# Eight of 26 embedding fields picked on chip in a four-tile interaction network, with a new tile schedule

## What is computed

```
e  = stack([tbl_f[ids[:, f]] for f in range(26)], axis=1)          # 512 x 26 x 32
x1 = einsum('bik,bjk,hij->bhk', e,  e, W1) + b1[None, :, None]     # 128 maps
x2 = einsum('bik,bjk,hij->bhk', x1, e, W2) + b2[None, :, None]     # 128 maps
z  = sum(concatenate([x1, x2], axis=1), axis=-1)                   # 512 x 256
h  = relu(concatenate([z, dense_ctx], axis=1) @ W_top1 + b_top1)   # 512 wide
h  = relu(h @ W_top2 + b_top2)                                     # 256 wide
y  = h @ W_top3                                                    # 512 x 1
```

## Time and profile before

| | |
|---|---|
| timed, median of 3 | 188.49 us |
| the profiled execution, span of the core | 269.0 us |
| PE busy, 1239 matmul records | 171.1 us |
| ACT / DVE / POOL busy | 103.7 / 94.1 / 109.4 us |
| mean granted TensorE clock | 0.797 |

### The profile page before, as it was taken

How to read it: one execution, slowest core, us unless ns; L and a number is a source line. 1 busy time by engine, 2 the same in 40 slices (tenths; PEclk the granted TensorE clock), 3 DMA queues, 4 the chain that set the end, 5 groups by cost and what they waited for, 6 DMA issues and landing times.

```text
span 269.0 us, 3544 instructions
## 1 busy us (share of the span) xinstructions
PE 171.1 (64%) x1239; PEld 158.7 (59%) x1239; DVE 94.1 (35%) x370; ACT 103.7 (39%) x267; POOL 109.4 (41%) x110
## 2 busy tenths in 40 slices
PE   7900594209929388986300799954001999899997
PEld 7800583209729287976300789954002999888985
DVE  0576003210943086920000568500003569047200
ACT  1020330019595165494000462951003463966313
POOL 3778777720077400577774003877770000000000
PEclk9975598556997869996555599995555799999999
DMA  6700011000001000011000000001000000000000
GB/s 240 250 12 13 12 14 14 13 7 0 0 10 17 11 1 4 2 12 15 14 12 10 0 0 2 11 12 15 12 12 2 0 0 0 0 0 0 0 0 3
DMA packets 5729, 5.08 MB, mean 19 GB/s; under 512 B 2875, under 2 KB 5061, under 8 KB 5718
## 3 DMA queue, kind: packets, MB, share of 16 engines
q0 software_dynamic: 3328, 1.71, 4.7%
q1 hardware_dynamic: 1698, 2.34, 2.6%
q10 hardware_dynamic: 692, 0.89, 1.0%
HBM read 4.93 MB, written 0.00 MB: 18 GB/s over the span
## 4 chain that ended last, share of the span: by engine, by line
PE 35%; another core or an unknown queue 30%; ACT 15%; DVE 9%; issue 9%; POOL 0%; DVEq 0%; ACTq 0%; POOLq 0%
PE bank L321 9%; ACT diag L467 8%; PE bank L287 4%; DVE t L650 4%; PE bank L322 4%; PE bank L281 4%; PE bank L256 3%; PE bank L332 2%; DVE prod L771 2%; PE bank L372 1%; ACT w2t L432 1%; ACT t L486 1%; DVE prod L616 1%; PE bank L275 1%
## 5 line engine op out<-in xcount | busy, mean ns | idle before, releaser
L242 POOL DMA_INDIRECT rows<-in_tbl_dram,idx x104 | 108.7, 1045 | 91.1 <-DVE prod L616 57.4
L321 PE MATMUL bank<-diag,prod 128*128 128x108 f32 x256 | 60.7, 336 | 56.0 <-DVE t L650 44.3
L321 PEld LDWEIGHTS bank<-diag,prod 128*128 128x128 f32 x256 | 46.6, 227 | 59.5 <-issue 59.5
L650 DVE COPY t<-bank 13x64 f32<-13x64 f32 (+2 forms) x128 | 26.7, 209 | 108.6 <-ACT t L487 66.7
L322 PE MATMUL bank<-diag,prod 128*77 128x64 f32 x256 | 41.7, 249 | 0.3 <-issue 0.3
L322 PEld LDWEIGHTS bank<-diag,prod 128*77 128x77 f32 x256 | 36.8, 173 | 0.5 <-issue 0.5
L485 ACT COPY t<-bank 55x128 f32<-55x128 f32 x32 | 8.3, 259 | 71.9 <-remote 47.8
L467 ACT COPY diag<-prod 32x416 f32<-32x416 f32 (+2 forms) x48 | 33.4, 696 | 1.0
L287 PE MATMUL bank<-w1ab,w2t 128*128 128x169 f32 x52 | 16.0, 489 | 14.6 <-ACT folded L434 9.7
L287 PEld LDWEIGHTS bank<-w1ab,w2t 128*128 128x128 f32 x52 | 12.8, 278 | 17.5 <-ACT folded L434 10.4
L281 PE MATMUL bank<-w1s,w2t 128*128 128x183 f32 x52 | 10.8, 377 | 16.4 <-ACT w2t L432 15.6
(11 more groups left out here) (79 smaller groups left out, 186.3 us busy)
## 6 DMA issues: line engine op xcount, KB each, us to landing
rows<-in_tbl_dram,idx POOLq DMA_INDIRECT x104
wt<-in_W_top_dram SPq DMA_DIRECT2D x2, 512.0 KB
w<-in_L_rec_W_dram ACTq DMA_DIRECT2D x1, 832.0 KB
w<-in_L_rec_W_dram SPq DMA_DIRECT2D x1, 832.0 KB
w<-in_L_rec_W_dram SPq DMA_DIRECT2D x1, 338.0 KB
idx<-in_ids_dram SPq DMA_DIRECT2D x4, 13.0 KB
vec<-in_L_rec_b_dram ACTq DMA_DIRECT2D x2, 0.5 KB
dctx<-in_dense_ctx_dram ACTq DMA_DIRECT2D x1, 32.0 KB
```

The source lines that it names most:

```text
L242: pool.indirect_dma_start(rows[:, f, :], None, tables[f], bass.IndirectOffsetOnAxis(ap=idx[i][:, f:f + 1], axis=0)).then_inc(s_got[part], 16)
L321: nc.tensor.matmul(m0[:, g * P:g * P + JW * QUADS], prod[:, G, 0:P], mov, start=True, stop=True)
L650: ins = nc.vector.tensor_copy(t1[p0:p0 + HALF, GRAM + slot:GRAM + slot + nb, n].rearrange("p j (g r) -> p j g r", r=QUADS), m1[64:64 + HAL ...
```

## The change

What it does:

- Fields are reordered (ORDER) so that eight fields with 1000 or 1250 rows stand at positions 0 to 3 and 13 to 16 (SMALL). They are no longer gathered. Their tables are loaded whole (`small`, 128 x 2240 floats, row number modulo 128 on the partitions). PE spreads the low seven bits of the ids over the partitions (`broadcast`, eight matmuls of 512 columns), DVE compares them with the partition number (`onehot`), and for each tile `look_up` multiplies one-hot by table, six banks a tile (widths 512, 512, 256, 320, 320, 320). DVE's `pick` multiplies each bank by a mask (`chosen`) and reduces over the 8 or 10 chunks into `rows[t]`.
- POOL gathers 18 fields a tile, 72 in all, into four separate buffers. It waits for nothing of DVE, but after every third gather (BURST), and at the end of a part, until they have landed.
- The weights come from memory in the layout that is needed (`w1p`, `w1t`, `w2t`, `vec`, `dctx` are permuted copies), so PE's transposes of `w2`, of `w1ab`, `w1s`, `vec` and `dctx` and DVE's strided sums go; one add gives `w1s` and one `z1w`.
- `diag` is laid out (group, quadrant, field) instead of (group, field, quadrant). For the first two parts ACT fills it over all 128 partitions with a per-partition scale of 0 or 1 (`spread`, four instructions a part); the third part is filled by DVE with four small copies.
- `factor`, a copy of the fields, lies in PSUM (bank 6), and the products read one factor from there.
- Moments go in four steps of eight groups over two sets of three banks, and are read out of PSUM with a stride of 32 or 16 floats (`evict`, `bands`).
- The loops are written out. The dense layers of tile t stand ahead of the moments of tile t + 1, which wait for `s_y`. Ahead of the last tile PE runs 12 matmuls that nobody reads (`keep_clock`).

The diff, cut to its core:

```diff
-GSTEP = 4
+GSTEP = 8
 STEPS = GROUPS // GSTEP
+GBANK = 4
+NBANK = GBANK * QUADS
 NSTEP = GSTEP * QUADS
+GPROD = 4
+PRODS = GROUPS // GPROD
 COL_A = P + 64
 COL_B = COL_A + HALF
 PCOLS = COL_B + HALF + WRAP
...
+SMALL = [0, 1, 2, 3, 13, 14, 15, 16]
+CHUNKS = [8, 8, 8, 8, 8, 10, 10, 10]
+MAXC = max(CHUNKS)
+SPLACE = [EMB * sum(CHUNKS[:e]) for e in range(len(SMALL) + 1)]
+PICKS = [(0, 2), (2, 4), (4, 5), (5, 6), (6, 7), (7, 8)]
+CROWS = P
+CBITS = 7
+NEEDS = [2, 6, 6]
+WARM = 6
+FILL = 12
 D_CTX = 16
...
-        MOM = [(bank[0], bank[1]), (bank[2], bank[3])]
-        Z1, Z2 = bank[4], bank[5]
-        L1 = [bank[6], bank[7], bank[2], bank[3]]
-        L2, L2_LAST = bank[6:8], bank[4:6]
-        L3 = bank[6]
-        s_w1, s_w2, s_vec, s_ctx, s_wt = (sem(n) for n in ("s_w1", "s_w2", "s_vec", "s_ctx", "s_wt"))
+        Z1, Z2 = bank[0], bank[7]
+        L1 = [bank[3], bank[4], bank[5], bank[7]]
+        L2, L3 = bank[0:2], bank[2]
+        ARRIVE = [[6, 7, 6, 7, 6, 7], [1, 2, 3, 4, 5, 1]]
+        LATE = [bank[3], bank[4], bank[5], bank[7]]
...
+            for t in range(TILES):
+                if t < 2:
+                    pool.wait_ge(s_idx[t], 16)
+                for part, (_, f1, _, g0) in enumerate(PARTS):
+                    for f in range(g0, f1):
+                        if f > g0 and (f - g0) % BURST == 0:
+                            pool.wait_ge(s_got[t][part], 16 * (f - g0))
+                        pool.indirect_dma_start(
+                            rows[t][:, f, :], None, tables[f],
+                            bass.IndirectOffsetOnAxis(ap=idx[:, t, f:f + 1], axis=0)).then_inc(s_got[t][part], 16)
+                    pool.wait_ge(s_got[t][part], 16 * (f1 - g0))
...
+            def broadcast():
+                pe.wait_ge(s_place, 1)
+                for e in range(len(SMALL)):
+                    nc.tensor.matmul(bank[e][:], with_dims(ident[0:len(SMALL), e:e + 1], (0, P)), placef[:],
+                                     start=True, stop=True).then_inc(s_bc, 1)
+            def look_up(t, picks):
+                for pick in picks:
+                    e0, e1 = PICKS[pick]
+                    ps = bank[ARRIVE[t > 0][pick]]
+                    if t == 0 and pick >= 2:
+                        pe.wait_ge(s_pick, pick - 1)
+                    elif t and pick == 5:
+                        pe.wait_ge(s_pick, t * len(PICKS) + 1)
+                    for e in range(e0, e1):
+                        c = slice(SPLACE[e] - SPLACE[e0], SPLACE[e + 1] - SPLACE[e0])
+                        mm = nc.tensor.matmul(ps[:, c], onehot[:, e, t * P:(t + 1) * P],
+                                              small[:, SPLACE[e]:SPLACE[e + 1]], start=True, stop=True)
+                    mm.then_inc(s_em, 1)
...
+                    b0 = 3 * (s % 2)
+                    if s == 1 and t:
+                        pe.wait_ge(s_h1, t * MT1)
                     if s >= 2:
                         pe.wait_ge(s_e0, t * STEPS + s - 1)
                         pe.wait_ge(s_eg, t * STEPS + s - 1)
                     for g in range(GSTEP):
                         G = s * GSTEP + g
-                        mov = diag[:, G, :, :].rearrange("p j r -> p (j r)")
-                        nc.tensor.matmul(m0[:, g * P:g * P + JW * QUADS], prod[:, G, 0:P], mov, start=True, stop=True)
-                        mm = nc.tensor.matmul(m1[0:M1, g * J1 * QUADS:(g + 1) * J1 * QUADS], prod[:, G, P:P + M1],
-                                              mov[:, JLOW * QUADS:], start=True, stop=True)
+                        if G % GPROD == 0:
+                            pe.wait_ge(s_pb, t * PRODS + G // GPROD + 1)
+                        m0 = bank[b0 + g // GBANK][:].rearrange("p (g r j) -> p g r j", g=GBANK, r=QUADS)
+                        m1 = bank[b0 + 2][0:M1, :].rearrange("p (g r j) -> p g r j", g=GSTEP, r=QUADS)
+                        nc.tensor.matmul(m0[:, g % GBANK, :, 0:JW], prod[:, G, 0:P], diag[:, G, :, :], start=True, stop=True)
...
+            broadcast()
+            for q in range(DONE["ctB"]):
+                make(q)
+            pe.wait_ge(s_oh, len(SMALL))
+            pe.wait_ge(s_small, 16)
+            look_up(0, (0, 1))
+            for q in range(DONE["ctB"], DONE["v1"]):
+                make(q)
+            look_up(0, (2, 3, 4, 5))
+            pe.wait_ge(s_sf, DONE["v1"])
+            for t in range(TILES):
+                if t:
+                    pe.wait_ge(s_y, t)
+                if t == TILES - 1:
+                    keep_clock(t)
                 moments(t)
+                if t < TILES - 1:
+                    pe.wait_ge(s_e0, t * STEPS + 3)
+                    pe.wait_ge(s_eg, t * STEPS + 3)
+                    look_up(t + 1, (0, 1))
+                pe.wait_ge(s_e0, t * STEPS + STEPS)
+                pe.wait_ge(s_eg, t * STEPS + STEPS)
+                if t == 0:
+                    for q in range(DONE["v1"], len(SETUP)):
+                        make(q)
+                    pe.wait_ge(s_sf, len(SETUP))
+                    pe.wait_ge(s_vec, 32)
+                    pe.wait_ge(s_wt, 48)
+                if t < TILES - 1:
+                    look_up(t + 1, (2, 3, 4))
+                z2_low()
+                if t < TILES - 1:
+                    look_up(t + 1, (5,))
+                z2_high()
+                if t == 0:
+                    pe.wait_ge(s_z1w, 1)
+                z1()
+                if t < TILES - 1:
+                    pe.wait_ge(s_pick, (t + 2) * len(PICKS))
+                layer1(t)
+                layer2(t)
+                layer3(t)
...
+            def evict(t):
                 for s in range(STEPS):
+                    b0 = 3 * (s % 2)
+                    act.wait_ge(s_mom, t * STEPS + s + 1)
+                    if s == 0 and t:
+                        act.wait_ge(s_z1, t)
+                    n0 = s * NSTEP
+                    def low(p0, p, slots, js):
+                        src = bank[b0 + 2][0:p, :].rearrange("p (n j) -> p j n", n=NSTEP)[:, js]
+                        dst = t1[p0:p0 + p, slots, n0:n0 + NSTEP]
+                        return nc.scalar.copy(dst, src)
+                    low(0, C1, slice(0, GRAM), slice(0, J1, 2))
+                    low(64, C1, slice(0, GRAM - 1), slice(1, J1 - 1, 2))
+                    low(0, C1, slice(GRAM, GRAM + 1), slice(J1 - 1, J1))
+                    for b in range(GSTEP // GBANK):
+                        src = bank[b0 + b][:].rearrange("p (n j) -> p j n", n=NBANK)[:, 0:JW]
+                        n = n0 + b * NBANK
+                        ins = nc.scalar.copy(t0[:, :, n:n + NBANK], src)
+                    ins.then_inc(s_e0, 1)
+            def spread(t, part):
+                f0, f1, col, _ = PARTS[part]
+                act.wait_ge(s_turn[part], t + 1)
+                for r in range(QUADS):
+                    ins = nc.scalar.activation(diag[:, :, r, f0:f1], prod[:, :, col:col + f1 - f0], ACT.Identity,
+                                               scale=quad[:, r:r + 1])
+                ins.then_inc(s_diag, 1)
...
+            for part in range(LATE_PART):
+                spread(0, part)
+            for t in range(TILES):
+                evict(t)
+                if t == 0:
+                    for q in range(DONE["v1"], len(SETUP)):
+                        take(q)
+                    act.wait_ge(s_vec, 32)
+                if t < TILES - 1:
+                    spread(t + 1, 0)
+                act.wait_ge(s_z2, t + 1)
+                nc.scalar.activation(z[1][:], Z2[:, 0:P], ACT.Identity, bias=b2x32[:, 0:1]).then_inc(s_z2s, 1)
+                act.wait_ge(s_z1, t + 1)
+                nc.scalar.copy(z[0][:], Z1[:, 0:P]).then_inc(s_z1s, 1)
                 relu1(t)
+                relu2(t)
+                copy_y(t)
+                if t < TILES - 1:
+                    spread(t + 1, 1)
...
+            def pick(t):
+                if t == 0:
+                    dve.wait_ge(s_ch, 1)
+                for i, (e0, e1) in enumerate(PICKS):
+                    n, cs = e1 - e0, CHUNKS[e0]
+                    width = n * EMB * cs
+                    dve.wait_ge(s_em, t * len(PICKS) + i + 1)
+                    if t or i:
+                        dve.wait_ge(s_sum, t * len(PICKS) + i)
+                    nc.vector.tensor_tensor(
+                        picked[:, 0:width].rearrange("p (f k c) -> p f k c", f=n, c=cs),
+                        bank[ARRIVE[t > 0][i]][:, 0:width].rearrange("p (f k c) -> p f k c", f=n, c=cs),
+                        with_dims(chosen[:, t, e0, 0:1], (MAXC, n), (0, EMB), (1, cs)), ALU.mult).then_inc(s_pick, 1)
+                    dve.wait_ge(s_pick, t * len(PICKS) + i + 1)
+                    nc.vector.tensor_reduce(rows[t][:, SMALL[e0]:SMALL[e0] + n, :],
+                                            picked[:, 0:width].rearrange("p (f k c) -> p f k c", f=n, c=cs),
+                                            mybir.AxisListType.X, ALU.add).then_inc(s_sum, 1)
...
```

(26 more changed lines are left out.)

635 lines of the change are left out of this document (280 added, 355 removed).

## The result

The changed kernel takes 201.57 us (median of 4 runs, 200.36 to 202.46), the kernel before 188.15 (187.78 to 188.94): a ratio of 1.070, 95% interval 1.064 to 1.076. The forecast was 208 us and slower. One fact is needed for all that follows: the kernel before takes 187 to 191 us on some chips and 268 to 278 us on others (24 timed runs on two of them), and its page shows an execution of the second sort; the changed kernel, timed above on a chip where before takes 188, hardly differs between them. Ratios and intervals compare the faster executions of both kernels, medians are over all of them, and among the 13 of the kernel before on the chip with 189.28 are two far outside, of 210.91 and 360.20 us, which stay unexplained.

The account below looks back on a forecast made before the run. PE's serial chain was taken to bound the changed kernel: first moments 52, tile 0 40.3, tiles 1 and 2 68.4, tile 3 31.3 and clock 7 give 199 us of span; with 8.5 outside, 208 us, range 186 to 221.

Parts of the forecast that it names:

- outside the span: Time of a timed execution beyond the profiled span: 3 to 13 us, taken as 8.5 and added at the end.
- A tile's chain: PE's serial work per tile, moments, eviction, look-ups, dense layers and spread: 34.2 us, against 31 for gathers.
- the clock's share: PE at half clock after idle between tiles: 0.6, 2, 2 and 2.5 us for tiles 0 to 3, 7 in all.
- The gathers: POOL's 72 gathers in bursts of three, 31 us a tile; fourth tile landed at about 134, not the bound.
- Strided reading of PSUM: ACT's copies out of PSUM at 128-byte step: nothing added; a doubling would be about 3.5 us a tile.
- Pick: VectorE's multiplies and reduces of looked-up rows: about 1.05 ns an element and 0.16 us an instruction, 7 us a tile.
- bare cover: ACT's spread of part 0 ends some 11.7 us after the moments, with z2 ready at about 12.4.
- The start: Work before the first moments, broadcast (7.6 us), folds, look-ups, transposes and last pick: first moments at about 52 us.
- reconstruction: Sum for the kernel before without the unnamed waits, 104 gathers in a row and then the last tile: 175 to 185 us.
- The unnamed waits: Waits for unnamed releasers in the kernel before, 47.8 us on ScalarE: taken as belonging to the profiled execution.
- Rival 3: Unnamed waits partly real, written-out loops and bursts of three remove them: 187 or less, results 176 to 190; chance 0.17.

Follow-up runs that it names:

- first two experiments: Changed kernel without POOL's waits for landed gathers: 277.77 us; kernel before with its four hardware loops written out: 268.98 us, ratio 0.994.
- the two runs with 9.4 us: Changed kernel with broadcast on 128 rows instead of 8: 194.16 us; that kernel with second spread and moments moved ahead of y: 187.57 us.

## Why the prediction came out as it did

The spans, cut at the first moment (us; the sum of the prediction beside four profiles):

| | first moment | to the end | outside the span | time |
|---|---|---|---|---|
| forecast | 52 | 147 | 8.5 | 208 |
| changed kernel | 56.46 | 144.1 | 1.8 | 202.43 |
| broadcast on 128 rows | 50.24 | 144.5 | 2.1 | 196.78 |
| and moments ahead of y | 50.16 | 135.0 | 2.1 | 187.26 |
| and no unread matmuls | 48.47 | 135.0 | 2.0 | 185.54 |

- **A tile's chain**: right, with the clock's share elsewhere than forecast. From moments to moments 38.05, 36.98 and 36.27 us (56.46, 94.51, 131.49, 167.76), forecast with the clock 40.9, 36.2 and 36.2; the last 32.8 against 31.3 + 2.5. After the second tile's last moment (109.96) the next came 21.5 us later, forecast 21.9, and VectorE's first product, begun 16.9 after (126.88), was ready after some 17.4, forecast 17.2. Half pace took 3.1 us at the start of the second tile and 1.7 at that of the third, where 2 each were added, and none at the start of the last, where 2.5 were; 1.7 behind the last eviction (the 4.80 above) had no term. The twelve unread matmuls stand in the third of the four stretches, not the last.
- **The gathers**: right. The last gather started at 133.80 and had landed at about 136.4, forecast 134; no transpose waits for rows. They are off the chain. A gather takes 0.965 on average against 1.045. The Trainium skill's shared port ("SBUF — State Buffer", section SBUF: two separate sides) would explain that by the factor in PSUM; but the kernel with 128 rows has the same factor and 1.020, the two last kernels 1.000 and 1.037, so it isn't shown.
- **Strided reading of PSUM**: nothing, as taken. The group of the copies in the changed kernel, against 512 ns in the kernel before, which reads runs of four floats:

```profile
L483 ACT COPY t<-bank 128x432 f32<-128x432 f32 x32 | 14.8, 515 | 0.0
```

- **Pick**: 0.69 us for 512 elements and 0.49 for 320, as forecast (1.05 ns each and 0.16), and bare cover held: `spread` of part 0 ended at 121.7, 0.39 us ahead of z2.
- **The start**: 4.5 us too early. The broadcast was priced at 7.6 by columns and took 14.0, and the first fold ran at the same half pace, +1.9; the experiment with 128 rows took 6.2 of it back. The rest of the start came 4 us sooner than summed.
- **Outside the span**: the term that failed, 8.5 against 1.8. It was worked out from the timed 188.49 and a reconstruction of a kernel that the profile showed differently (175 to 185). Every run of every kernel in the experiments has 1.7 to 2.2. The upper end, 185, is what agrees with it: 185 + 1.8 = 187. There is no profile of the kernel before where it takes 188, so how its time is made up stays open.
- **The unnamed waits**: the wrong reading. They were taken as belonging to the profiled execution only. They are in every timed run too (268.3 to 272.2 us on the first chip), on chips where a row of gathers holds the others up. Rival 3 had the mechanism but not its place: it made the changed kernel 176 to 190, where the waits that it takes away belong to the other chips; and of its two causes the loops are worth at most 1.2% and the bursts of three 74 us (first two experiments). Its sum doesn't add up either: with 3 outside and starts 10 us earlier, 199 + 3 - 10 is 192, not 187. That this reading did no harm is luck: both kernels were timed on a chip where before stays at 188, and there the sign is as forecast; on the others the change is a gain of a quarter.
- That 208 came within 3% is in part luck too, since errors of both signs cancel: +4.5 in the start, -3 in the tiles, -6.7 outside, 208 to 202.

## What to carry to other kernels

A row of indirect gathers may hold up the other engines' waits, and how much depends on the chip: compare a profile's span with the timed median before reading it, and where they differ by more than some 2 us ask for the spans of timed runs, don't price a remainder. Three gathers and a wait for their landing made a kernel that takes the same time on both kinds of chip (201.6 and 203.5, later 187.6 and 186.4), at the price of 1.4 to 1.6 us a wait, which a kernel pays in full once they make gathers its bound (the kernel before, 189 to 253). A stretch of 2.35 us without matmuls cost 4.0 and 5.5 us here, since four or eight groups behind it ran at half pace: ask of each wait at a tile's turn whether it protects anything, because moving two of them gave 6.6 us by the medians and made the kernel slightly faster than before.

## What the runs showed of the hardware that was not expected

- Where the kernel before takes 269 to 274 us, waits are passed on late while indirect gathers are issued back to back, not from the first on but after some six in a row of nine and some 15 in the row of 72: two fp32 matmuls (1.59 us), then 9.6 us of standing; full pace once they end. It shows on PE, ScalarE and VectorE alike, with the DMA engines at 8 to 9%. What carries it (a queue, a path of the semaphores) isn't known, nor why it shows on one kind of chip in every run; that it can't be much on the other follows from the kernel before, 104 gathers in 188 us, and was not profiled.
- A matmul whose moving operand has 8 rows took 1.75 us for 512 columns (14.02 / 8), twice what full pace gives, with the granted clock at 1.00 in the record, and so did the 128-row fold behind it until about 22 us. PE in the same stretch of the changed kernel, and of the one without unread matmuls, where it has 128 rows:

```profile
8.00:10.00 2.00, 2.00 (x3) 0.66 (x2) 0.75 (x1) 0.00 (x0) 0.00 (x0) 1.00 1.03 407
```

```profile
8.00:10.00 2.00, 2.00 (x6) 0.84 (x5) 2.00 (x4) 0.00 (x0) 0.00 (x0) 1.00 1.08 422
```

  Three records against six in the same 2 us and under the same DMA load. The column of the granted clock doesn't show this slowdown; the count of records does. On the chip of the two runs with 9.4 us, PE had four records in that stretch, also under 1.00, and six from 10 us on, so rows aren't all of it. The kernel with all fields gathered and paced has no broadcast on that chip; its first fold, behind 4.91 us in which PE stands, takes as long as the fold behind the 8-row matmuls (10.13), while behind 128-row ones it takes 8.22:

```profile
9.27 10.08 PE L291 MATMUL bank<-w1s,w2t 128*128 128x183 f32 x52 [4.91 <-DMA w2t<-in_w2t_dram]
```

  So in these runs PE is slow early behind 8-row matmuls and behind standing alike, with the granted clock at 1.00 all the while; what sets its pace is open.
- Reading PSUM with a stride of 128 bytes instead of in runs of four floats costs ScalarE nothing: 515 ns against 512.
